# A two-layer decoder on one core: unrolled expert slots of 47 tiles, norms in two parts, and the store inside the combining stage

## The chip, the cores and the metric

The kernel runs on one core of a Trainium2 chip. The metric is the device time of one execution in microseconds, the median of the runs. TensorE's full clock is 2.4 GHz, and the profile gives the granted share of it.

## The reference, cut to what matters

The input `x` is 4 batches of 512 tokens with 512 features. Six sublayers follow one another, each added to its input and layer-normed: causal attention, cross attention, a ternary-weight feed-forward net, causal attention again, a graph layer, and a mixture of experts. The last two are what the change touches.

```
# graph layer (L1_xattn), added to x, then the norm
sim  = (h Wq)(h Wk)^T scaled;  thr = 153rd largest of each row
A    = sigmoid(sim) * (sim >= thr);  A = (A + A^T) / 2
x    = layernorm(x + (1 - gamma) * x + gamma * A)
# mixture of experts (L1_ffn), 16 experts of width 256, top 2
combine[n, e] = the two renormed shares of token n
for e in range(16):
    out += combine[:, e] * ((silu(x Wu[e]) * (x Wg[e])) @ Wd[e])
out += shared expert;  x = layernorm(x + out)
```

## The kernel before

`X` holds the 2048 tokens in SBUF as 16 tiles of 128 tokens by 512 features. `build` runs the stages one after another; each is a block in which every engine has its own instruction list in program order, with semaphores between the engines, and each ends with a barrier.

**The graph stage** (`stage_graph`) ends with a loop over the 4 batches. ScalarE makes four sigmoids (line 1546) and scales four tiles of X (1550); VectorE masks (1584); TensorE transposes the masked tiles (1522); VectorE adds tile and transpose (1591), adds that to X (1597) and takes the moments with `bn_stats` (1600). After the loop VectorE runs the 25 small dependent steps of `emit_rstd` (lines 64 to 77) for all 16 tiles at once, and then norms the 16 tiles (1605).

**The expert stage** (`stage_experts`) has three parts. `route_and_share` sorts the tokens by expert into tiles of 128 rows that each belong to one expert, and computes the shared expert. At most `SLOT_TILES` = 48 such tiles are there, and all of them are computed. `run_slots` runs over these 48 slots. For each one, GpSimd issues two indirect DMAs, of the tokens (`XG`, 128 rows of 2 KB, line 1986) and of the expert's weights (`RAW`, 128 rows of 12 KB, line 1988). Every fp32 product is made of three fp32r products: ScalarE copies the high part (`WH`, `XTH`, `HH`), an engine subtracts it from the raw value to get the low part (`WL`, `XTL`, `HL`), and TensorE multiplies high by high, low by high and high by low. The low part of the up weights comes in two halves: VectorE does the first (2089), GpSimd the second (1993). In one slot TensorE does 8 up products (2144), the 2 transposes of H of the slot before (2159), the last 4 up products, the 4 transposes of the next slot's tokens (2132), and the 6 down products of the slot before (2178).

The order of the other engines in turn t is: GpSimd waits until VectorE has copied the two row numbers of slot t+3 into `PICK` (2080, 2081) and until `down_lo` of slot t-1, issues the two DMAs of slot t+3, and subtracts for slot t+1. VectorE copies the row numbers, subtracts for the up weights of t+1, and makes `HL` of t-1 (2104), `XTL` of t+1 (2085), `H` of t (2109), the copy of the result `YS` of t-1 out of PSUM (2118) and the low part of the down weights of t (2121). ScalarE copies the up weights of t+1 (2060), `HH` of t-1 (2064), `XTH` of t+1 (2036), takes the silu of t (2069) and copies the down weights of t (2072). SyncE stores `YS` to `y_rows` in HBM (2027). RAW, XG and YS are rings of 4 buffers, the other tiles rings of 2 or 1. The first 4 and the last 5 turns are written out, and the 40 between them are a hardware loop (`Fori`) of 4 turns.

**`combine_slots`** gathers for each of the 16 token tiles the two result rows by indirect DMA (2207, a ring of 4), and VectorE adds them to X with their shares (2216) and takes the moments (2219); then come the 25 steps and the 16 norms (2224), all on VectorE. After the barrier `store_x` writes X with one 4 MB DMA (2268).

Of the kernel before, what the change touches and what calls it, by code (L numbers as in the profile page):

```python
# [4 lines left out]
F32 = mybir.dt.float32  # L5
# [8 lines left out]
P = 128  # L14
NB = 4
# [64 lines left out]
def emit_rstd(nc, step, stats, mean, var, y, a):  # L80

    for inst in rstd_steps(nc, stats, mean, var, y, a):
        step(inst)

# [1385 lines left out]
def stage_graph(nc, X, C, A, GR):  # L1470
# [10 lines left out]
    with ctx:  # L1481
# [16 lines left out]
        mean, var, rstd, tmp = (small(n, NTILE) for n in ("mean", "var", "rstd", "tmp"))  # L1498
# [3 lines left out]
                 "sigm xs masked turned summed halved z_done stat norm between")  # L1502
# [24 lines left out]
        def _(act):  # L1527
# [14 lines left out]
            with act.Fori(0, NB) as b:  # L1542
                act.wait_ge(q["masked"], b * NT)
                act.sem_inc(q["between"], 1)
                for i in range(NT):
                    ac.activation(SIGM[:, i, :], SIM[:, b * NT + i, :], ACT.Sigmoid).then_inc(q["sigm"], 1)
                act.wait_ge(q["z_done"], b * NT)
                act.sem_inc(q["between"], 1)
                for i in range(NT):
                    ac.activation(XS[:, i, :], XF[:, b * NT + i, :], ACT.Identity, scale=g2[:, 0:1]).then_inc(q["xs"], 1)  # L1550

        @block.vector
        def _(dve):
# [26 lines left out]
            with dve.Fori(0, NB) as b:  # L1580
                dve.wait_ge(q["turned"], b * 2)
                for i in range(NT):
                    dve.wait_ge(q["sigm"], b * NT + i + 1)
                    ve.scalar_tensor_tensor(out=L[:, i, :], in0=SIM[:, b * NT + i, :], scalar=low[:, bass.ds(b * NT + i, 1)],  # L1584
                                            in1=SIGM[:, i, :], op0=ALU.is_ge, op1=ALU.mult).then_inc(q["masked"], 1)
                for v in range(2):
                    dve.wait_ge(q["turned"], b * 2 + v + 1)
                    dve.wait_ge(q["masked"], b * NT + NT)
                    if v == 0:
# [11 lines left out]
            dve.wait_ge(q["stat"], NTILE)  # L1601
            fin = Steps(dve, q["norm"], 0, RSTD_STEPS + NTILE)
# [4 lines left out]
            fin.done()  # L1607

def stage_experts(nc, X, C, A):  # L1610
# [7 lines left out]
    SLOT_TILES = 2 * NTILE + NE  # L1618
    ctx = ExitStack()
    with ctx:  # L1620
# [13 lines left out]
        combine_slots(nc, X, T)  # L1634
# [289 lines left out]
def run_slots(nc, X, C, A, T, F, SLOT_TILES):  # L1924

    RING = 4
    TURNS = SLOT_TILES // RING  # L1930
    UGW, DW = KC * 2 * F, 2 * D
    pe, ve, ac, gp = nc.tensor, nc.vector, nc.scalar, nc.gpsimd
    ctx = ExitStack()
    with ctx:
# [4 lines left out]
        def places(n, count, w, dtype):  # L1939
# [5 lines left out]
        YS = places("YS", RING, D, F32)  # L1945
        PICK = places("PICK", RING, 2, U32)
# [13 lines left out]
        q = {n: sem(n) for n in ("picked xt_full x_hi x_lo up_hi down_hi up_lo up_lo_pool down_lo "  # L1960
                                 "u_full silu_done h_made ht_full h_hi h_lo y_full y_taken between").split()}
        x_in, w_in, y_out = ([sem(f"{n}{i}") for i in range(RING)] for n in ("x_in", "w_in", "y_out"))

# [5 lines left out]
        def run(eng, step):  # L1969

            for i in range(RING):
                step(i, i)
            with eng.Fori(1, TURNS - 1) as j:
                for i in range(RING):
                    step(j * RING + i, i)
            for i in range(RING + 1):
                step((TURNS - 1) * RING + i, i)

        def has(t, lo, hi):
            return not isinstance(t, int) or lo <= t <= hi  # L1980

        @block.gpsimd
        def _(pool):
            def fetch(t, i):
                i = i % RING
                pool.indirect_dma_start(out=XG[i], out_offset=None, in_=T["x_rows"],  # L1986
# [361 lines left out]
```

## Time and profile before

| | |
|---|---|
| median of 3 runs | 2813.01 us (2809.75 to 2814.63) |
| the profiled execution: its own time | 2814.64 us |
| its span | 2812.7 us, 34294 instructions |
| TensorE busy, matmuls | 2066.3 us (73%) |
| its instructions | 12308 matmuls, 12308 weight loads |
| VectorE busy | 1822.6 us (65%) |
| ScalarE busy | 1217.9 us (43%) |
| GpSimd busy | 801.8 us (29%) |
| DMA, mean over the span | 95 GB/s |
| mean granted clock of TensorE | 0.858 |

The span is cut by stages: the graph loop and its norms lie at 2078 to 2150 us, routing and the shared expert at 2150 to 2389, the 48 slots at 2389 to 2736, the combination at 2736 to 2799, and the store at 2800 to 2813. The shares of busy time are means over stages with different limits; the rows that follow are read stage by stage. A busy time counts what the engine spent in its instructions, a wait for a shared resource included.

### The profile page before, as it was taken

Reading aid. Unit: us, or ns where it says so; the run is one execution under the profiler, and the core shown is the slowest. Engines: PE = TensorE matmul, PEld = TensorE weight load, DVE = VectorE, ACT = ScalarE, POOL = GpSimd, SP = SyncE. Lnnn points to the kernel's source line nnn. Section 1 sums busy time; section 2 is a strip of 40 time slices with the busy share of each in tenths; the row PEclk is TensorE's granted clock in tenths of the full one; section 3 lists DMA queues with packets and bytes.
Section 4 is the critical chain, followed back from the end, with each engine's and each line's share of the span. In section 5 each row is a group of like instructions: output and inputs, shape, how many; then the busy total and the mean of one; then the engine's idle time right before and its main releaser. Section 6 shows DMA issues by size and latency. Waiting matters only on the chain. (4 is left out here: it accounts for less than half of the span.)

```text
span 2812.7 us, 34294 instructions
## 1 busy us (share of the span) xinstructions
PE 2066.3 (73%) x12308; PEld 1398.0 (50%) x12308; DVE 1822.6 (65%) x2851; ACT 1217.9 (43%) x2168; POOL 801.8 (29%) x712
## 2 busy tenths in 40 slices
PE   5999997386877886899847999994014589677760
PEld 4778775122222223555526777772003477555540
DVE  3456555476767757899963555654885433788876
ACT  2332222285556563677762322321862021556540
POOL 1211322106577511121111212131000130666654
PEclk8999998589889888999967999997555599999995
DMA  4422221655244204000013223221002000899965
GB/s 142 98 56 59 57 58 23 180 173 144 90 127 121 61 12 170 1 1 1 1 38 98 64 50 69 52 62 60 0 0 107 1 1 0 308 307 303 305 223 164
DMA packets 84875, 266.48 MB, mean 95 GB/s; under 512 B 17488, under 2 KB 19024, under 8 KB 73600
## 3 DMA queue, kind: packets, MB, share of 16 engines
q0 software_dynamic: 29856, 153.33, 18.2%
q1 hardware_dynamic: 53856, 111.01, 13.9%
q8 instruction: 89, 1.46, 0.2%
q10 hardware_dynamic: 1024, 0.26, 0.0%
q14 instruction: 50, 0.41, 0.0%
HBM read 171.70 MB, written 41.99 MB: 76 GB/s over the span
## 5 line engine op out<-in xcount | busy, mean ns | idle before, releaser
L875 DVE TENSOR_REDUCE x_negm<-x_M 128x2 f32<-128x1024 f32 x256 | 309.3, 1223 | 115.4 <-PE x_M L935 114.9
L824 ACT ACTIVATE x_PT<-x_T 128x512 f32<-128x512 f32 x512 | 280.2, 598 | 210.8 <-PE x_T L955 206.0
L317 ACT ACTIVATE L_attn_PT<-L_attn_T 128x512 f32<-128x512 f32 x320 | 175.4, 595 | 357.9 <-PE L_attn_T L519 357.7
L387 DVE TENSOR_REDUCE L_attn_negm<-L_attn_M 128x2 f32<-128x1024 f32 (+1 forms) x192 | 191.8, 1041 | 56.5 <-PE L_attn_M L500 56.2
L224 POOL DMA_DIRECT2D L_attn_QKS<-L_attn_HL x64 | 34.9, 546 | 598.0 <-ACT L_attn_HL L302 564.3
L955 PE MATMUL x_T<-x_QS,x_KS 49*128 49x512 f32 x512 | 144.0, 559 | 64.0 <-ACT x_PT L824 43.7
L517 PE MATMUL L_attn_T<-L_attn_QKS 97*128 97x256 f32 (+3 forms) x512 | 164.6, 383 | 10.2 <-DMA L_attn_QKS<-L_attn_mT 7.9
L964 PE MATMUL x_O<-x_PT,x_V 128*32 128x512 f32 x1024 | 160.7, 704 | 7.6 <-issue 7.6
L955 PEld LDWEIGHTS x_T<-x_QS,x_KS 49*128 49x128 f32 x512 | 53.0, 204 | 217.5 <-ACT x_PT L824 135.9
L935 PE MATMUL x_M<-x_KS,x_QS 48*128 48x512 f32 x512 | 120.7, 468 | 42.8 <-DMA x_QS<-x_xl 23.3
L498 PE MATMUL L_attn_M<-L_attn_QKS 96*128 96x384 f32 (+2 forms) x384 | 134.8, 420 | 19.2 <-DVE L_attn_XTL L361 11.5
L1522 PE MATMUL graph_P<-ident,graph_L 128*128 128x128 f32 x64 | 15.7, 428 | 173.0 <-DVE graph_L L1584 167.8
L2060 ACT ACTIVATE slots_WH<-slots_RAW 128x1024 fp32r<-128x1024 f32 x94 | 94.6, 1054 | 100.3 <-DMA slots_RAW<-in_experts,slots_PICK 100.3
L2121 DVE TENSOR_TENSOR slots_WL<-slots_RAW,slots_WH 128x1024 fp32r<-128x1024 f32 x48 | 130.9, 2726 | 0.2 <-ACT slots_WH L2072 0.2
L434 PE MATMUL L_attn_M<-L_attn_XTH,L_attn_WH 128*128 128x512 f32 x256 | 109.1, 426 | 16.3 <-DVE L_attn_XTL L361 16.3
L519 PE MATMUL L_attn_T<-mask_kq,identr 128*128 128x128 f32 x512 | 120.4, 247 | 0.0
L1993 POOL TENSOR_TENSOR slots_WL<-slots_RAW,slots_WH 128x1024 fp32r<-128x1024 f32 x48 | 116.3, 2423 | 10.5 <-ACT slots_WH L2060 5.6
L1534 ACT ACTIVATE graph_seen_a<-graph_SIM,graph_mid 128x512 bf16<-128x512 f32 x128 | 90.5, 708 | 59.1 <-DMA graph_SIM<-graph_sim 39.8
L517 PEld LDWEIGHTS L_attn_T<-L_attn_QKS 97*128 97x128 f32 x512 | 104.8, 205 | 17.0 <-DMA L_attn_QKS<-L_attn_mT 9.1
L405 DVE RECIPROCAL L_attn_AQ<-L_attn_DEN 128x512 f32<-128x512 f32 x32 | 107.2, 3349 | 7.1 <-PE L_attn_O L537 7.1
L434 PE MATMUL L_attn_M<-L_attn_XTH,L_attn_WL 128*128 128x512 f32 x256 | 106.4, 416 | 0.0
L1986 POOL DMA_INDIRECT slots_XG<-moe_x_rows,slots_PICK x48 | 48.6, 1012 | 201.7 <-DVE slots_PICK L2081 200.9
(377 smaller groups left out, 5711.9 us busy)
## 6 DMA issues: line engine op xcount, KB each, us to landing
L_attn_QKS<-L_attn_HL SPq DMA_DIRECT2D x192, 128.0 KB, 4.7
L_attn_QKS<-L_attn_HL POOLq DMA_DIRECT2D x192, 128.0 KB, 4.1
moe_y_rows<-slots_YS SPq DMA_DIRECT2D x48, 256.0 KB, 7.6
x_WRAW<-in_w_gateT POOLq DMA_DIRECT2D x8, 1024.0 KB, 7.5
x_QS<-x_xh SPq DMA_DIRECT2D x128, 64.0 KB, 2.4
x_WRAW<-in_w_upT POOLq DMA_DIRECT2D x8, 1024.0 KB, 5.6
x_WRAW<-in_w_downT POOLq DMA_DIRECT2D x8, 1024.0 KB, 5.9
ffn_w<-x_WTER POOLq DMA_DIRECT2D x12, 512.0 KB, 3.6
```

The source lines that it names most:

```text
L317: ac.activation(PT[:, s, bank], T[:, bank], ACT.Exp, scale=SCALE).then_inc(t_free, 1)
L387: last = ve.tensor_reduce(negm[:, g % 2, h0:h0 + nh, i], src, AX.X, ALU.max, negate=True)
L434: inst = pe.matmul(out, lhs(a, k), rhs(a, k), start=(n == 0), stop=(n == len(passes) - 1))
L498: pe.matmul(m[:, c:c + w], QKS[0:R, r, 0, h, P * i:P * (i + 1)], QKS[0:R, r, 1, h, 0:w], start=True, stop=False)
L517: pe.matmul(T[:, c:c + w], QKS[0:R + 1, r, 1, h, P * j:P * (j + 1)], QKS[0:R + 1, r, 0, h, P * j:S], start=True, stop=False)
L519: last = pe.matmul(T[:, c:c + P], C["identr"][:], C["mask_kq"][:], start=False, stop=True)
L824: ac.activation(PT[:, s // 4, head(s), :], T[(STEPS_S * g + s) % 3][:], ACT.Exp, scale=SCALE).then_inc(t_free, 1)
L875: ve.tensor_reduce(negm[:, g % 2, u // 4:4:2, u % 4], m[:].rearrange("p (r k) -> p r k", r=2), AX.X, ALU.max, negate=True).then_inc(m_free, 1)
L935: last = pe.matmul(m[:, BANK * r:BANK * (r + 1)], QS[rows, g % 4, u // 4, P * (u % 4):P * (u % 4 + 1)], KS[rows, g % KV, :], start=True, s ...
L955: pe.matmul(T[(STEPS_S * g + s) % 3][:], KS[rows, g % KV, P * j:P * (j + 1)], QS[rows, g % 4, head(s) % 2, :], start=True, stop=True).then ...
L964: last = pe.matmul(O[VW * h:VW * (h + 1), :], V[:, (g // KV) % 2, j, g % KV, :], PT[:, j, h, :], start=(j == 0), stop=(j == NT - 1))
L2121: ve.tensor_tensor(WL[i % 2][:, DOWN], RAW[i][:, DOWN], WH[i % 2][:, DOWN].bitcast(F32), ALU.subtract).then_inc(q["down_lo"], 1)
```

## The change

- `run_slots`: the loop is written out for all slots, and `SLOT_TILES` is 47. GpSimd only issues DMAs; the row numbers are taken in place from `slot_token` and `weight_row`, without `PICK`. RAW and XG are rings of 6, and slot t is fetched once slot t-6 has been read (`down_lo`, `up_lo`). VectorE does both halves of the up weights' low part. ScalarE copies the result out of PSUM (`take_y`). SyncE's stores have constant addresses.
- `stage_graph`: the loop over batches is written out; the moments of the first 12 tiles are turned into mean, rstd and `shift` = -mean*rstd inside the last batch, those of the last 4 tiles at the end. ScalarE norms the first 14 tiles and VectorE the last 2.
- `combine_slots`: the same in two parts, and SyncE stores each batch once it is normed, the last one in two halves of 0.5 MB. `store_x` isn't called any more.

```diff
@@ stage_graph
+            for b in range(NB):
...
+                if b == NB - 1:
+                    moments(0, 0, EARLY)
...
-            emit_rstd(nc, fin, stats[:], mean[:], var[:], rstd[:], tmp[:])
-            for t in range(NTILE):
-                fin(ve.tensor_scalar(XF[:, t, :], XF[:, t, :], mean[:, t:t + 1], rstd[:, t:t + 1],
-                                     ALU.subtract, ALU.mult))
+            moments(1, EARLY, NTILE)
+            last = Steps(dve, q["between"], 0, NT // 2)
+            for t in range(EARLY + NT // 2, NTILE):
+                last(ve.tensor_scalar(XF[:, t, :], XF[:, t, :], mean[:, t:t + 1], rstd[:, t:t + 1],
+                                      ALU.subtract, ALU.mult))
@@ run_slots
-    RING = 4
+    RING, LAST = 6, SLOT_TILES - 1
@@ run_slots, GpSimd
+            for t in range(SLOT_TILES):
+                n = t % RING
+                if t >= RING:
+                    pool.wait_ge(down_lo, t - RING + 1)
+                    pool.wait_ge(up_lo, 2 * (t - RING + 1))
+                pool.indirect_dma_start(out=XG[n], out_offset=None, in_=T["x_rows"],
+                                        in_offset=bass.IndirectOffsetOnAxis(T["slot_token"][:, t:t + 1], 0)
+                                        ).then_inc(x_in[n], 16)
+                pool.indirect_dma_start(out=RAW[n], out_offset=None, in_=weights,
+                                        in_offset=bass.IndirectOffsetOnAxis(T["weight_row"][:, t:t + 1], 0)
+                                        ).then_inc(w_in[n], 16)
@@ run_slots, ScalarE
+            for t in range(SLOT_TILES + 2):
+                if t < LAST:
+                    up_weights(t + 1)
+                if 1 <= t <= SLOT_TILES:
+                    act.wait_ge(ht_full, t)
+                    ac.activation(HH[:], HT[:, 0:F], ACT.Copy).then_inc(h_hi, 1)
+                if t >= 2:
+                    take_y(t - 2)
+                if t < LAST:
+                    turned(t + 1)
+                if t <= LAST:
+                    act.wait_ge(u_full, t + 1)
+                    ac.activation(SU[t % 2], U[t % 2][:, 0:F], ACT.Silu).then_inc(silu_done, 1)
+                    if t >= 2:
+                        act.wait_ge(y_full, t - 1)
+                    ac.activation(WH[t % 2][:, DOWN], RAW[t % RING][:, DOWN], ACT.Copy).then_inc(down_hi, 1)
@@ run_slots, VectorE
+            for t in range(SLOT_TILES + 1):
+                if t < LAST:
+                    up_rest(t + 1, 0)
+                if t >= 1:
+                    dve.wait_ge(h_hi, t)
+                    ve.tensor_tensor(HL[:], HT[:, 0:F], HH[:].bitcast(F32), ALU.subtract).then_inc(h_lo, 1)
+                if t < LAST:
+                    up_rest(t + 1, 1)
+                    turned_rest(t + 1)
+                if t <= LAST:
+                    dve.wait_ge(silu_done, t + 1)
+                    ve.tensor_tensor(H[t % 2], SU[t % 2], U[t % 2][:, F:], ALU.mult).then_inc(h_made, 1)
+                    dve.wait_ge(down_hi, t + 1)
+                    ve.tensor_tensor(WL[t % 2][:, DOWN], RAW[t % RING][:, DOWN], WH[t % 2][:, DOWN].bitcast(F32),
+                                     ALU.subtract).then_inc(down_lo, 1)
@@ combine_slots, VectorE
             for t in range(NTILE):
+                if t == EARLY:
+                    moments(0, 0, EARLY)
...
+            moments(1, EARLY, NTILE)
+            for t in range(EARLY + NT // 2, NTILE):
+                ve.tensor_scalar(XF[:, t, :], XF[:, t, :], mean[:, t:t + 1], rstd[:, t:t + 1],
+                                 ALU.subtract, ALU.mult).then_inc(applied_v, 1)
@@ combine_slots, ScalarE
+            act.wait_ge(shifted, 1)
+            for t in range(EARLY):
+                norm_tile(t)
+            act.wait_ge(shifted, 2)
+            for t in range(EARLY, EARLY + NT // 2):
+                norm_tile(t)
@@ combine_slots, SyncE
+            for b in range(NB - 1):
+                sp.wait_ge(applied_a, NT * (b + 1))
+                sp.dma_start(out[:, b, :, :], X[:, b, :, :]).then_inc(x_out, 16)
+            sp.wait_ge(applied_a, EARLY + NT // 2)
+            sp.dma_start(out[:, NB - 1, 0:NT // 2, :], X[:, NB - 1, 0:NT // 2, :]).then_inc(x_out, 16)
+            sp.wait_ge(applied_v, NT // 2)
+            sp.dma_start(out[:, NB - 1, NT // 2:, :], X[:, NB - 1, NT // 2:, :]).then_inc(x_out, 16)
```

`EARLY` is 12. `moments(part, lo, hi)` waits for the `bn_stats` of tiles below `hi`, runs `emit_rstd` and one more step, `emit_shift`, on tiles `lo` to `hi`, and releases ScalarE. `norm_tile(t)` is one activation with scale `rstd` and bias `shift`, in place. TensorE's order in a slot stays as it was.

## Rows read from the trace of the kernel before

**Rows 1.** Windows: length, busy PE PEld DVE ACT POOL, PEclk, DMA share, GB/s.
```profile
2403.00:2407.00 4.00, 4.00 (x12) 3.10 (x12) 1.10 (x1) 2.01 (x2) 2.78 (x4) 0.60 1.01 427
2407.00:2411.00 4.00, 2.50 (x14) 1.90 (x13) 2.56 (x7) 3.27 (x5) 2.34 (x1) 1.00 1.01 390
2430.00:2700.00 270.00, 209.61 (x944) 157.12 (x944) 236.69 (x316) 159.85 (x236) 169.33 (x118) 1.00 0.91 305
2801.00:2811.00 10.00, 0.00 (x0) 0.00 (x0) 0.00 (x0) 0.00 (x0) 0.00 (x0) 0.50 1.03 386
```

**Rows 2.** Waits of the engines from 2430 to 2700 us.
```profile
ACT slots_WH L2060 <- DMA slots_RAW<-in_experts,slots_PICK: 87.4, 39, 3.4
...
PE slots_Y L2178 <- DVE slots_HL L2104: 42.0, 39, 1.2
...
PE slots_U L2144 <- POOL slots_WL L1993: 18.2, 40, 0.5
```

**Rows 3.** Timeline of one slot: start, us, engine, line, operation.
```profile
2562.89 0.98 POOL L1986 DMA_INDIRECT slots_XG<-moe_x_rows,slots_PICK  x1 [2.20 <-DVE slots_PICK L2081]
...
2564.18 0.95 POOL L1988 DMA_INDIRECT slots_RAW<-in_experts,slots_PICK  x1 [0.30 <-issue]
...
2565.15 2.38 POOL L1993 TENSOR_TENSOR slots_WL<-slots_RAW,slots_WH 128x1024 fp32r<-128x1024 f32 x1
...
2565.72 2.90 DVE L2121 TENSOR_TENSOR slots_WL<-slots_RAW,slots_WH 128x1024 fp32r<-128x1024 f32 x1
...
2568.55 0.14 DVE L2080 COPY slots_PICK<-moe_slot_token 128x1 uint32 x1
```

**Rows 4.** Groups by form, 2430 to 2700 us: busy, mean ns, idle before.
```profile
L2089 DVE TENSOR_TENSOR slots_WL<-slots_RAW,slots_WH 128x1024 fp32r<-128x1024 f32 x40 | 48.4, 1210 | 0.0
...
L2118 DVE COPY slots_YS<-slots_Y 128x512 f32<-128x512 f32 x39 | 27.0, 692 | 33.1 <-PE slots_Y L2178 33.1
...
L2036 ACT ACTIVATE slots_XTH<-slots_XT 128x512 fp32r<-128x512 f32 x40 | 23.8, 595 | 22.7 <-PE slots_XT L2132 22.3
```

**Rows 5.** Timeline: TensorE's first up products of slots 1, 2 and 47.
```profile
2409.20 1.17 PE L2144 MATMUL slots_U<-slots_WH,slots_XTH 128*128 128x512 f32 x4 [1.50 <-DVE slots_XTL L2085]
...
2414.33 1.16 PE L2144 MATMUL slots_U<-slots_WH,slots_XTH 128*128 128x512 f32 x4
...
2722.15 1.09 PE L2144 MATMUL slots_U<-slots_WH,slots_XTH 128*128 128x512 f32 x4
```

**Rows 6.** DMA issues, 2430 to 2700 us; last number: median us to landing.
```profile
slots_RAW<-in_experts,slots_PICK POOLq DMA_INDIRECT x39, 9.3
```

**Rows 7.** The tile YS over the whole span: landing of its stores.
```profile
DMA to landing us min/median/max: 2.0/7.6/9.6
```

**Rows 8.** The page's third part: instruction blocks fetched by DMA.
```profile
q8 instruction: 89, 1.46, 0.2%
```

**Rows 9.** Timeline of the combination and the store.
```profile
2770.93 1.54 DVE L2216 SCALAR_TENSOR_TENSOR X<-combine_YG,moe_share,X 128x512 f32<-128x512 f32 x2 [0.31 <-DMA combine_YG<-moe_y_rows,moe_slot]
...
2772.50 0.69 DVE L2219 BATCH_NORM_STATS2 combine_stats<-X 128x6 f32<-128x512 f32 x1
...
2783.69 0.69 DVE L2219 BATCH_NORM_STATS2 combine_stats<-X 128x6 f32<-128x512 f32 x1
...
2799.90 0.39 SPq L2268 DMA_DIRECT2D out_x<-X  x1
```

**Rows 10.** Timeline of the last batch of the graph stage and its norms.
```profile
2120.47 2.56 ACT L1550 ACTIVATE graph_XS<-X,graph_g 128x512 f32 x4 [7.86 <-DVE X L1597]
2121.15 2.74 DVE L1584 SCALAR_TENSOR_TENSOR graph_L<-graph_SIM,graph_low,graph_SIGM 128x512 f32<-128x512 f32 x4
...
2126.02 1.23 DVE L1591 TENSOR_TENSOR graph_SUM<-graph_P,graph_L 128x1024 f32<-128x1024 f32 x1 [2.13 <-PE graph_P L1522]
...
2134.83 0.18 DVE L64 TENSOR_TENSOR graph_mean<-graph_stats 128x16 f32<-128x16 f32 x1
...
2140.08 9.28 DVE L1605 TENSOR_SCALAR X<-X,graph_mean,graph_rstd 128x512 f32<-128x512 f32 x16
```

More of the change, by code:

```diff
@@ L83, in emit_rstd, with emit_shift @@
         step(inst)
+def emit_shift(nc, step, mean, rstd, shift):
+    step(nc.vector.scalar_tensor_tensor(out=shift, in0=mean, scalar=-1.0, in1=rstd, op0=ALU.mult, op1=ALU.mult))
 def moment_steps(nc, t, z):
@@ L1944, in run_slots @@
         XG = places("XG", RING, D, F32)
[L1945 to L1946 removed]
+        YS = places("YS", 4, D, F32)
         WH = places("WH", 2, UGW + DW, F32R)
@@ L2018, in _ @@
         @block.sync
         def _(sp):
-            def step(t, i):
-                if has(t, 1, SLOT_TILES):
-                    sp.wait_ge(q["y_taken"], t)
-                    if not isinstance(t, int):
-                        sp.sem_inc(q["between"], 1)
-                    n = (i - 1) % RING
-                    rows = slice(P * (t - 1), P * t) if isinstance(t, int) else bass.ds((t - 1) * P, P)
-                    sp.dma_start(T["y_rows"][rows], YS[n]).then_inc(y_out[n], 16)
-            run(sp, step)
@@ L2073, in _, with up_weights, turned, take_y @@
-            run(act, step)
+            def up_weights(t):
+                act.wait_ge(w_in[t % RING], 16 * (t // RING + 1))
+                if t >= 2:
+                    act.wait_ge(u_full, t - 1)
+                for part in PARTS:
+                    ac.activation(WH[t % 2][:, part], RAW[t % RING][:, part], ACT.Copy).then_inc(up_hi, 1)
+            def turned(t):
+                act.wait_ge(xt_full, t + 1)
+                ac.activation(XTH[t % 2], XT[:], ACT.Copy).then_inc(x_hi, 1)
+            def take_y(t):
+                act.wait_ge(y_full, t + 1)
+                if t >= 4:
+                    act.wait_ge(y_out[t % 4], 16 * (t // 4))
+                ac.activation(YS[t % 4], Y[t % 2][:], ACT.Copy).then_inc(y_taken, 1)
@@ L2123, in _, with turned_rest, up_rest @@
-            run(dve, step)
+            def turned_rest(t):
+                dve.wait_ge(x_hi, t + 1)
+                ve.tensor_tensor(XTL[t % 2], XT[:], XTH[t % 2].bitcast(F32), ALU.subtract).then_inc(x_lo, 1)
+            def up_rest(t, part):
+                dve.wait_ge(up_hi, 2 * t + part + 1)
+                cols = PARTS[part]
+                ve.tensor_tensor(WL[t % 2][:, cols], RAW[t % RING][:, cols], WH[t % 2][:, cols].bitcast(F32),
+                                 ALU.subtract).then_inc(up_lo, 1)
@@ L2180, in step, with combine_slots @@
                             n += 1
-                    last.then_inc(q["y_full"], 1)
-            run(t_, step)
-def combine_slots(nc, X, T):
+                    last.then_inc(y_full, 1)
+def combine_slots(nc, X, T, out):
     NTILE, RING = NB * NT, 4
-    ve = nc.vector
+    EARLY = NTILE - NT
+    ve, ac = nc.vector, nc.scalar
     ctx = ExitStack()
@@ L2296, in build @@
             if s == "M":
-                stage_experts(nc, X, C, A)
-        store_x(nc, X, out.rearrange("b (i p) d -> p b i d", p=P))
+                stage_experts(nc, X, C, A, out_rows)
+        if "M" not in stages:
+            store_x(nc, X, out_rows)
 def layout(inputs):
```

301 lines of the change are left out of this document (111 added, 190 removed).

## The prediction, made before the changed kernel ran

> **What bounds the kernel now.** I read the page's slices first, then the stages by window, then the waits, the timeline and the groups of the slot loop. The stages run one after another, so each is its own problem, and three are touched. The big one is the 48 slots. TensorE goes from slot 1's first up product at 2409.20 to slot 47's at 2722.15 [rows 5], 46 steps of 6.80 us; from 2430 to 2700 a slot takes 6.87 us, which makes 39.3 of them. No resource is full there: in 270 us TensorE is busy 209.6, ScalarE 159.9, and VectorE 236.7 in name only [rows 1]. The timeline shows what paces it [rows 3]. GpSimd waits 2.20 us for VectorE's PICK, issues two DMAs (0.98 and 0.95), and subtracts for 2.38 us, until 2567.53. VectorE's down subtract begins inside that time and takes 2.90 us, though the same shape takes 1.21 on line 2089 [rows 4]; it ends at 2568.62, just 1.1 us after GpSimd's. So it is held until GpSimd is done, and costs 1.69 more. The next PICK starts at 2568.55, and GpSimd's next issue waits for it. That is a ring through two engines: PICK, two issues, GpSimd's subtract, VectorE's held subtract, PICK. TensorE pays for it with 42.0/39 = 1.08 us a slot waiting for HL, which stands behind VectorE's held work, and 18.2/40 = 0.46 for GpSimd's half [rows 2]. ScalarE's 87.4/39 = 2.2 us of waiting for RAW [rows 2] is the same ring seen from the DMA: RAW is issued late and lands 9.3 us after its issue [rows 6].
>
> **The slots, part by part.** GpSimd's subtract, PICK and the hold go; the ring is cut. What limits next?
> TensorE: its list is unchanged. 6.87 - 1.08 - 0.46 = 5.33 us, and the step from slot 1 to slot 2, before the hold sets in, took 2414.33 - 2409.20 = 5.13 [rows 5]. Floor 5.13.
> VectorE: 236.69/39.3 = 6.02 us a slot [rows 1]; less the hold 1.69, the YS copy 0.69 [rows 4] and two picks (about 0.2 [rows 3]); plus one subtract of 1.21 [rows 4]: 4.65.
> ScalarE: 159.85/39.3 = 4.07 [rows 1], plus `take_y`. That form isn't in the trace; XTH is the same size from PSUM, 0.595 [rows 4]: 4.66. From below it can't be free, from above VectorE's copy is 0.69.
> GpSimd: 0.98 + 0.95 + two gaps of 0.30 = 3.2 at most, with nothing behind it but itself.
> DMA: a slot moves 305 GB/s x 6.87 us = 2.095 MB [rows 1]. With three weight loads queued the engines moved 427 and then 390 GB/s, the big store 386 [rows 1]: 4.91, 5.37 and 5.43 us a slot.
> With the ring of 6, slot t is fetched when slot t-6 is done, some five slots ahead of use, so the 9.3 us of landing hide, and the DMA queues never run dry. So TensorE (5.13) and the DMA (about 5.4) are the next bounds, and VectorE and ScalarE have 0.5 us of slack each. The latter matters: HL now stands behind one unheld subtract of 1.21, and XTL behind HL and the second one. The path from TensorE's transposes of H through HH, HL, the second subtract and XTL to the next up products is about 0.4 + 0.4 + 0.4 + 1.2 + 0.7 us, which is as long as TensorE's own work in that time (5.13 less the 8 up products at about 0.23 each). It fits with nothing to spare. I take 5.45 us, from the sustained DMA rates; the ends are 5.13 and, below, 6.25.
> Steps: before 46 x 6.80 = 312.95; after 45 x 5.45 = 245.25 (one slot less). **Gain 67.7 us.** The first slot is paced by its weights and the half clock of TensorE as before, and the last one's tail stays: nothing for both. SyncE's stores keep their order; they are hidden behind three slots of the ring.
> The unrolling itself I price at nothing: the first four turns and the last five were written out already, and the step from slot 1 to 2, in that part, is the fastest. What it costs if that fails is a rival.
>
> **The combination and the store.** Tile 11 is added from 2770.93 and its moments end at 2773.19 [rows 9]. Then come `moments(0)`, 26 dependent steps. In the graph stage 25 of them took 2140.08 - 2134.83 = 5.25 [rows 10], so 26 take 5.46: until 2778.65. Four tiles of 1.54 + 0.69 = 2.23 follow; their gathers were issued meanwhile, since the ring of 4 doesn't wait for them: 2787.6, against 2784.38 before. `moments(1)`: 2793.1. Then VectorE norms two tiles at 9.28/16 = 0.58 [rows 10] while ScalarE does two at 2.56/4 = 0.64 [rows 10]: both end by 2794.4. ScalarE's 12 early tiles (7.7 us from 2778.7) end at 2786.4, under VectorE's adding, and each batch's 1 MB (2.7 us at 386 GB/s) is stored by 2790. What is left behind 2794.4 is 1 MB: 2.7 us, plus a fixed part. The 4 MB store went from 2799.90 to the span's end at 2812.7, 12.8 us, of which 4.19 MB at 386 GB/s is 10.9; so 1.9 is fixed. The barrier between the last norm (about 2799.0) and the issue, 0.9 us, now lies behind the store. 2794.4 + 0.1 + 2.7 + 1.9 + 0.9 = 2800.0 to 2800.6 with the second issue. **Gain 12.2 us.**
>
> **The graph stage.** Its last mask ends at 2123.89. 26 steps: 2129.35, of which 2.13 us filled VectorE's wait for TensorE [rows 10]. From the first sum at 2126.02 to the steps at 2134.83 are 8.8 us, so 2138.2; `moments(1)` 2143.6; two norms 2145.0, against 2149.36. ScalarE's 12 tiles lie under it (2129.4 to 2137.1). **Gain 4.4 us.** The written-out loop gains nothing: no gap stands between batches on VectorE.
>
> **Sum.** 67.7 + 12.2 + 4.4 = 84.3. The profiled execution (span 2812.7, own time 2814.64) would come to a span of 2728.4 and a time of 2730.3; against the median of 2813.01 that is **2728.7 us**.
>
> **Rivals.**
> *Reads and writes together don't reach 386 GB/s.* In the even part the DMA share was already 0.91 at 305 GB/s [rows 1]. If those packets are as slow with full queues, the limit is 305/0.91 = 335 GB/s, a slot takes 6.25 us, the slots gain 312.95 - 281.3 = 31.7, and the time is 2813.0 - 48.3 = 2765. For it: the 386 and 390 were rates of writes alone and reads alone. The trace has gone over it, 427 and 390 GB/s in [rows 1].
> *The stores starve.* A YS store lands in 2.0 us when nothing else moves and in 7.6 as a rule [rows 7]: it waits behind weight packets. If a store has to wait for all that is queued, then with a ring of 6 that is 5 x 1.835 MB at 390 GB/s, 23.5 us, plus 2.0. YS has 4 places, so a slot can't go below 25.5/4 = 6.4 us: gain 25 + 16.6, 2771. Before, at most one or two loads were queued, so the trace can't exclude it. The skill (the same page, Queues, rings and completion order) says that an engine alternates between queues packet by packet; by that rule the store waits for one load's share and this rival falls.
> *The ring isn't the bound.* Another cycle over the engines, such as the tight path above, keeps the step at 6.8. Then one slot less (6.8), 0.15 or so, and 16.6: 2789. Against it: the 5.13 us step.
> *Slower.* The written-out lists have to be fetched. 89 blocks of 16.4 KB were [rows 8], mostly under low DMA load. If they are TensorE's, 1.46 MB over its 24,616 instructions (the table) is an estimate of 59 B each; with 48 a slot (2 x 944/39.3 [rows 1]), 47 slots are 8 blocks. If each is fetched only when needed, and waits for the whole backlog of 23.5 us, that is 8 x 23.5 = 188 us: 2917. It decides from 84.3/8 = 10.5 us a block. Against it: no stall shows at blocks fetched so far, so they come ahead of need, and a block lasts nearly six slots.
>
> **How the numbers follow.** The forecast (5.13 to 5.75 us a slot, 2714 to 2742) gets 0.60, the slow DMA (2742 to 2769) 0.22, starving stores 0.09, the unmoved bound 0.05, slower 0.04. The lower end of the range is the TensorE floor less 2 us for the two tails: 2712. Upward, 2762 leaves out the slowest third of the second case and the three others, about 0.2 in all. A measurement of this kernel can tell from no change what exceeds about 0.2%, 5.6 us: faster 0.95, same 0.01, slower 0.04.
>
> **What would show it.** After, VectorE's down subtract takes 1.21 us, not 2.90. TensorE's first up products come 5.45 us apart, and its waits for HL and GpSimd's half shrink from 1.54 to about 0.3 us. DMA runs at some 385 GB/s with a share near 1; if the share is 1 at 335 to 350 GB/s the second case holds; if ScalarE waits in `take_y` for a store, the third; if TensorE has idle time of 10 us with a q8 block in it, the last. The span ends about 30 us after the combination's tile 11 is added, not 42. The prediction is wrong if VectorE and ScalarE, with half a microsecond of slack, delay each other more than TensorE's list can hide.

## The result, and the profile after

The changed kernel takes **2701.65 us** (median of 4 runs, 2691.3 to 2702.86) against 2813.82 (4 runs, 2809.75 to 2814.71): 112 us less by the medians. The ratio of the runs, 0.9616 with a 95% interval of 0.9594 to 0.9638, makes it 108 us (102 to 114). The forecast was 2729, with a range of 2712 to 2762. The direction held, and so did what the prediction said of the kernel before; but the next bound was TensorE's own list and not the DMA, the gain was 28 us more than forecast (24 by the ratio), and the time lies below the range. All medians here are of executions in the usual, fast state; one of the four of "after, half on GpSimd" took 3019.73 us at a granted clock of 0.701 and is left out.

The profiled execution took 2691.3 us (span 2689.6), the fastest of the four. Part of its lead is not the change's: TensorE's first instruction of the graph stage starts at 2066.18 us and before at 2082.94, and all stages ahead of it are the same code. In the 14 traces of this study with that same code it starts anywhere from 2066 to 2088, and TensorE's mean granted clock up to there lies between 0.860 and 0.873. So the parts are read as lengths between two instructions of the same stages. In the last column is what the prediction's steps give.

| part | before | after | gain | forecast |
|---|---|---|---|---|
| graph stage, TensorE's first to next stage's first | 67.47 | 60.18 | 7.3 | 4.4 |
| routing and shared expert | 243.50 | 241.46 | 2.0 | 0 |
| slot 1 to the last slot, first up products | 312.95 | 230.97 | 82.0 | 67.7 |
| slot 0 to 1, and last slot to the end of its YS copy | 16.31 | 14.92 | 1.4 | 0 |
| first gather to the end of the span | 77.06 | 63.57 | 13.5 | 12.2 |
| sum | | | 106.2 | 84.3 |

The sum of 106 lies inside the interval of 102 to 114; the 2 us to the ratio's 108 and the 6 to the medians' difference are no more than the untouched stages vary.

The slots first. These are the windows of the kernel after that answer to [rows 1] (after the window and its length come the busy times of PE, PEld, DVE, ACT and POOL, then the granted clock, the DMA share and GB/s):

```profile
2377.00:2400.00 23.00, 21.29 (x96) 16.26 (x95) 19.62 (x24) 18.63 (x27) 10.44 (x9) 0.95 1.02 423
2400.00:2580.00 180.00, 177.59 (x844) 135.72 (x843) 172.14 (x211) 161.06 (x246) 101.97 (x71) 1.00 1.01 417
2580.00:2600.00 20.00, 19.72 (x95) 15.02 (x94) 19.09 (x25) 17.82 (x28) 8.34 (x6) 1.00 1.00 413
```

TensorE is busy 177.6 us of 180 instead of 209.6 of 270, and the DMA moves 417 GB/s for 180 us on end. Its first up products of slots 1, 2 and 46, for [rows 5]:

```profile
2382.67 1.16 PE L2101 MATMUL slots_U<-slots_WH,slots_XTH 128*128 128x512 f32 x4 [1.50 <-DVE slots_XTL L2058]
...
2387.81 0.47 PE L2101 MATMUL slots_U<-slots_WH,slots_XTH 128*128 128x512 f32 x1
...
2613.64 0.47 PE L2101 MATMUL slots_U<-slots_WH,slots_XTH 128*128 128x512 f32 x1
```

That is 230.97 us for 45 steps, 5.13 each, and every one is between 5.11 and 5.14. The waits from 2400 to 2580 us, all of them, against [rows 2]:

```profile
POOL slots_XG L2001 <- DVE slots_WL L2082: 69.3, 36, 1.9
ACT slots_XTH L2027 <- PE slots_XT L2092: 17.1, 35, 0.5
PEld slots_U L2101 <- issue: 16.5, 35, 0.5
POOL slots_RAW L2004 <- issue: 10.7, 35, 0.3
DVE slots_WL L2082 <- ACT slots_WH L2052: 7.1, 35, 0.2
```

No wait of TensorE's matmuls is left in the list, and ScalarE no longer waits for RAW. What stands first, GpSimd's 1.9 us a slot, is the wait for a place in the ring; nobody is late for it, since five further slots are already loaded or on their way. The groups of the same stretch, for [rows 4]:

```profile
L2063 DVE TENSOR_TENSOR slots_WL<-slots_RAW,slots_WH 128x1024 fp32r<-128x1024 f32 x71 | 86.4, 1217 | 0.0
...
L2001 POOL DMA_INDIRECT slots_XG<-moe_x_rows,moe_slot_token x36 | 60.6, 1684 | 69.3 <-DVE slots_WL L2082 69.3
L2082 DVE TENSOR_TENSOR slots_WL<-slots_RAW,slots_WH 128x1024 fp32r<-128x1024 f32 x35 | 42.9, 1226 | 7.1 <-ACT slots_WH L2052 7.1
L2004 POOL DMA_INDIRECT slots_RAW<-in_experts,moe_weight_row x35 | 42.7, 1219 | 10.7 <-issue 10.7
...
L2033 ACT ACTIVATE slots_YS<-slots_Y 128x512 f32<-128x512 f32 x35 | 20.8, 594 | 0.0
```

VectorE's down subtract takes 1.23 us, not 2.90, and the result's copy 0.594 on ScalarE (forecast 0.595). Now GpSimd pays: its issues take 1.68 and 1.22 us, where they took 0.98 and 0.95 [rows 3].

The combination, for [rows 9]:

```profile
2661.01 1.54 DVE L2183 SCALAR_TENSOR_TENSOR X<-combine_YG,moe_share,X 128x512 f32<-128x512 f32 x2 [0.67 <-DMA combine_YG<-moe_y_rows,moe_slot]
...
2668.90 8.57 ACT L2195 ACTIVATE X<-X,combine_shift,combine_rstd 128x512 f32<-128x512 f32 x12 [46.71 <-DVEq L2176]
...
2677.04 0.69 DVE L2186 BATCH_NORM_STATS2 combine_stats<-X 128x6 f32<-128x512 f32 x1
...
2683.01 1.52 ACT L2195 ACTIVATE X<-X,combine_shift,combine_rstd 128x512 f32<-128x512 f32 x2 [5.53 <-DVEq L2176]
...
2684.97 0.47 SPq L2213 DMA_DIRECT2D out_x<-X  x1
```

From tile 11's addition to the end it is 28.6 us instead of 41.8.

### The profile page after: what moved, and what is told of

It is laid out like the page before. It is cut to its first block and busy times, and to the rows that moved or that the text cites. A ratio compares the mean times of both kernels' runs of the same rounds, so it can differ in the third digit from the quotient of the medians.

```text
span 2689.6 us, 33324 instructions
## 1 busy us (share of the span) xinstructions
PE 2040.0 (76%) x12284; PEld 1381.2 (51%) x12284; DVE 1763.9 (66%) x2775; ACT 1257.8 (47%) x2237; POOL 719.8 (27%) x662
## 5 line engine op out<-in xcount | busy, mean ns | idle before, releaser
L960 PE MATMUL x_T<-x_QS,x_KS 49*128 49x512 f32 x512 | 143.1, 555 | 60.2 <-ACT x_PT L829 43.3
L2001 POOL DMA_INDIRECT slots_XG<-moe_x_rows,moe_slot_token x47 | 75.4, 1605 | 188.3 <-POOLq L48 104.2
L2063 DVE TENSOR_TENSOR slots_WL<-slots_RAW,slots_WH 128x1024 fp32r<-128x1024 f32 x94 | 114.3, 1218 | 13.4 <-ACT slots_WH L2023 13.4
L524 PEld LDWEIGHTS L_attn_T<-mask_kq,identr 128*128 128x128 f32 x512 | 105.0, 205 | 0.2
```

Of the source, the lines that this page charges most:

```text
L524: last = pe.matmul(T[:, c:c + P], C["identr"][:], C["mask_kq"][:], start=False, stop=True)
L960: pe.matmul(T[(STEPS_S * g + s) % 3][:], KS[rows, g % KV, P * j:P * (j + 1)], QS[rows, g % 4, head(s) % 2, :], start=True, stop=True).then ...
L2063: ve.tensor_tensor(WL[t % 2][:, cols], RAW[t % RING][:, cols], WH[t % 2][:, cols].bitcast(F32), ALU.subtract).then_inc(up_lo, 1)
```

## The experiments

The experiments ran in three groups, each on one chip with its own runs of the kernel before; that median stands in the third column, and times of different groups are compared by ratios and by lengths in the traces alone. "Step" is always the mean from slot 1's first up product to the last slot's. "Fewer products" and "tokens fetched twice" have two executions each, so they are read by their steps.

| kernel | time, us | before in its group | step, us | ratio to before, 95% |
|---|---|---|---|---|
| before | 2813.82 | | 6.80 | |
| after | 2701.65 | 2813.82 | 5.13 | 0.9594 to 0.9638 |
| slots only | 2725.28 | 2804.03 | 5.13 | 0.9671 to 0.9747 |
| combination only | 2792.02 | 2804.03 | | 0.9942 to 0.9982 |
| graph stage only | 2800.58 | 2804.03 | | 0.9943 to 0.9988 |
| slot loop written out only | 2805.17 | 2804.03 | 6.85 | 0.9972 to 1.0017 |
| half to VectorE only | 2790.09 | 2811.93 | 6.34 | 0.9901 to 0.9967 |
| after, half on GpSimd | 2749.98 | 2811.93 | 6.27 | 0.9759 to 0.9853 |
| after, rings of 4 | 2735.80 | 2811.93 | 6.08 | 0.9695 to 0.9770 |
| after, YS copy on VectorE | 2704.86 | 2811.93 | 5.26 | 0.9592 to 0.9660 |
| after, rings of 5 | 2728.67 | 2831.19 | 5.12 | 0.9608 to 0.9650 |
| after, fewer products | 2717.57 | 2831.19 | 4.94 | 0.9551 to 0.9634 |
| after, tokens fetched twice | 2752.46 | 2831.19 | 5.74 | 0.9693 to 0.9738 |
| graph loop written out only | 2829.16 | 2831.19 | 6.81 | 0.9969 to 1.0004 |

### The three parts, each alone

Each is the kernel before with one function taken from the kernel after.

```diff
-    SLOT_TILES = 2 * NTILE + NE
+    SLOT_TILES = 2 * NTILE + NE - 1
```

> The kernel before with the new run_slots and 47 slots; graph stage, combination and final store as before. Theory A: the three parts are independent, so this part has what the slots gained in the full change: a step of 5.13 us between TensorE's first up products (the length of TensorE's own list), 312.95 - 45 x 5.13 = 82 us from slot 1 to the last, 1.2 more in the tail; in all about 83 us less than before, to about 2730. Theory B, as the prediction had it: the DMA paces at 5.45 us, 68 us less, and the rest of the surplus came from elsewhere. Theory C: the shorter combination and graph stage help the slots too, and this kernel gains clearly less than the 97 us that slots, combination and store gained together less 13.4.

Measured: 231.01 us from slot 1 to the last, 5.13 a step; the ratio of 0.9709 makes 82 us less (71 to 92). Theory A. The slots' 5.13 doesn't depend on the other parts.

> The kernel before with only the combination changed: 12 tiles' moments early, norms on ScalarE for 14 tiles, each batch stored as it is normed, no 4 MB store at the end. The prediction said 12.2 us less; by the trace of the kernel after, first gather to the end of the span went from 77.0 to 63.6, 13.4 less. Theory A: 12 to 13.5 us less. Theory B, part of those 13.4 belongs to a shorter tail of the slots or to another state of the gathers: under 11.

Measured: from the first gather to the end of the span 63.65 us, before 77.06: 13.4 less. The time's own interval, 5 to 16 us less, can't separate the theories, the length can. Theory A.

> The kernel before with only the graph stage changed: loop over the batches written out, norms in two parts on two engines. The prediction said 4.4 us less, with nothing from writing out the loop; the trace after shows the stage 7.3 us shorter. Theory A: 7 us less, of which some 0.8 us for each of the four batches is from the written-out loop. Theory B: 4.4 less, and the rest of the 7.3 is how TensorE's clock fell in that stage.

Measured: the graph stage takes 60.2 us, as in the full change, so 7.3 less; the ratio makes the whole kernel 10 us less (3 to 16). What made up the 7.3 is taken apart by the last experiment.

### Is it the loop, the subtract or the ring?

```diff
-            for i in range(RING):
-                step(i, i)
-            with eng.Fori(1, TURNS - 1) as j:
-                for i in range(RING):
-                    step(j * RING + i, i)
-            for i in range(RING + 1):
-                step((TURNS - 1) * RING + i, i)
+            for t in range(SLOT_TILES + 1):
+                step(t, t - RING * min(t // RING, TURNS - 1))
```

> The kernel before with the 40 looped slots written out and nothing else: still 48 slots, rings of 4, the row numbers copied to PICK, GpSimd's half of the subtract. Theory A, the ring PICK, two issues, GpSimd's subtract, VectorE's held subtract is the pace: the step stays at 6.8 us and the time within 6 us of before. Theory B, the loop itself (waits against counted registers, its branch) sets a part of the pace, as the graph stage's shorter batches suggest, some 0.1 us for each wait: then the step falls by 0.2 to 1 us, 8 to 40 us less.

Measured: step 6.85, ratio 0.9995. Theory A: writing the slots out gives nothing by itself. The mean is 0.05 us higher than before because of a few slow steps, one of 9.61 us with a late load; the median step is 6.85 in both.

The second takes GpSimd's half away from it, in the kernel before:

```diff
@@ GpSimd
-                if has(t, 0, SLOT_TILES - 2):
-                    rest(t + 1, i + 1)
@@ VectorE, after HL of t-1
+                    up_rest2(t + 1, i + 1)
```

> The kernel before with one thing changed: GpSimd's half of the subtract of the up weights goes to VectorE. The loop, PICK, the rings of 4, 48 slots and the YS copy on VectorE stay. Theory A, VectorE's subtract was held by GpSimd's, and this closed the ring: with both on VectorE its work is 6.02 - 1.69 + 1.21 = 5.54 us a slot, its subtracts take 1.21 us each, and the step falls from 6.80 to about 5.55, 59 us less, with VectorE now the bound. Theory B, the late issues (PICK, ring of 4) are a bound of their own: RAW still arrives late, the step stays above 6.3.

Measured: step 6.34, 18 us less than before (9 to 28). VectorE's subtracts do take 1.21 us, so the hold is gone, but the step is far from theory A's 5.55 and just above the 6.3 of theory B. Theory B. The single steps swing between 5.4 and 9.6 us, and the loads come late:

```profile
ACT slots_WH L2052 <- DMA slots_RAW<-in_experts,slots_PICK: 90.3, 42, 4.1
```

These are 2.15 us a slot from 2430 to 2700 us, as much as in [rows 2]. So a second bound stood right behind the first. Whether it is PICK or the depth of the ring, this run doesn't tell; the rings of 4 below show that the depth alone is such a bound.

The third is the opposite: rings of 6 and no PICK as in the kernel after, and GpSimd subtracts again.

```diff
+            for t in range(SLOT_TILES + RING - 1):
+                if t >= RING - 1:
+                    rest(t - RING + 1)
@@ VectorE
-                    up_rest(t + 1, 1)
```

> The kernel after with GpSimd doing the second half of the subtract again; rings of 6, no PICK, written out. GpSimd: 0.98 + 0.95 + 0.3 + 2.38 = 4.6 us a slot, VectorE 4.65 - 1.21 + 1.69 = 5.1 if its subtract is held as before, and nobody is above TensorE's 5.13 by much. Theory A, the hold costs only where GpSimd's issue hangs on VectorE: with the ring cut the step is 5.13 to 5.5 us, 0 to 17 us more than after. Theory B, the hold alone makes the path through HL and XTL too long: 5.8 or more, over 30 us more than after.

Measured: step 6.27, 1.14 above after, and over 6 from the first steps on; 53 us above after by the ratios (0.9806 against 0.9616). Theory B. The groups from 2430 to 2580 us:

```profile
L1999 POOL TENSOR_TENSOR slots_WL<-slots_RAW,slots_WH 128x1024 fp32r<-128x1024 f32 x24 | 62.1, 2589 | 0.5
L2074 DVE TENSOR_TENSOR slots_WL<-slots_RAW,slots_WH 128x1024 fp32r<-128x1024 f32 x24 | 55.4, 2307 | 0.0
L2091 DVE TENSOR_TENSOR slots_WL<-slots_RAW,slots_WH 128x1024 fp32r<-128x1024 f32 x23 | 50.3, 2185 | 4.1 <-ACT slots_WH L2063 3.6
```

The hold now falls on either of VectorE's two subtracts, and both average over 2.1 us against 1.2. No load is late here, though the DMA moves 332 GB/s at a share of 0.94. The Trainium skill (SBUF — State Buffer, Who interferes with whom) says that VectorE and GpSimd share one pair of SBUF ports, that a VectorE instruction with both inputs in SBUF contends for it with a GpSimd instruction that reads SBUF, and that the one that comes second waits until the first is done. By that rule the hold is there as long as both subtract, and the trace agrees: 2.2 to 2.3 us instead of 1.2.

The fourth is the kernel after with `RING = 4` in place of 6.

> The kernel after with RAW and XG rings of 4 in place of 6. In the kernel after RAW lands 10.8 us (16.7 at most) after its issue. With 4 places a load is issued at most 3 slots ahead of its use, less the time in which the slot is read: 15.4 - 5.1 = 10.3 us at a step of 5.13. Theory A: a shorter queue also shortens the landing (9.3 us before), the step stays at 5.13 and the time within 4 us of after. Theory B: the landing doesn't fit, some slots wait for RAW, the step is 5.4 to 6.2, 12 to 50 us more than after.

Measured: step 6.08, theory B: 42 us more over the slots, and 33 by the ratio (0.9733 against after's 0.9616). Steps of 5.13 alternate with steps of up to 9.4. First the window and the waits from 2430 to 2580 us, then the DMA in 40 slices from 2470 to 2492 us:

```profile
2430.00:2580.00 150.00, 132.90 (x594) 100.46 (x594) 120.88 (x149) 112.42 (x173) 62.22 (x49) 0.96 0.93 341
...
ACT slots_WH L2023 <- DMA slots_RAW<-in_experts,moe_weight_row: 24.9, 18, 4.3
...
GB/s 246 261 320 331 421 410 406 406 473 413 447 358 425 421 458 439 387 469 424 350 317 183 89 115 153 305 246 0 156 443 469 417 421 465 417 324 302 249 373 216
```

The queue runs dry: the slices from 2481.5 to 2486 us have 0 to 305 GB/s, after GpSimd has waited 6.3 us for a place. RAW lands 9.9 us after its issue in the median (7.9 to 11.1), and the packets are slower as well: 0.93 of the engines' time for 341 GB/s, against 1.01 for 417 with full queues, 13% more time a byte. On paper 4 places are enough (9.9 for the landing, 2.3 from the release to RAW's issue, some 6.5 of use in the kernel after, which is 18.7 of 4 x 5.13 = 20.5), so there is some 2 us to spare for a transfer that swings by 3. That this swing is what uses it up is a reading of these rows and not shown by a run of its own. What is shown is the price of the depth: 6.08 against 5.13 us a step, with neither PICK nor hold in either kernel.

The same with `RING = 5`:

> The kernel after with rings of 5 for RAW and XG. With 4 places the queue ran dry in most slots, the step was 6.05 and the time about 34 us over after. Theory A, the pace is a matter of places times the step against load, wait and use of a place: one place more adds 5.13 us for a landing of 9 to 11 us, the queue never runs dry, and the step is 5.13, the time within 3 us of after. Theory B, the landing time grows with the depth (11.8 us at 6), so that 5 places still leave stalls: 5.2 to 5.5, 3 to 17 us over after.

Measured: step 5.12, and the window is full again, 148.0 us of TensorE in 150:

```profile
2430.00:2580.00 150.00, 148.00 (x705) 113.31 (x704) 143.51 (x176) 134.56 (x205) 84.42 (x59) 1.00 1.01 409
```

Theory A: five places do it, the sixth gives nothing. (The traces have 6.08 where the expectation says 6.05, and a median landing of 10.9 us where it says 11.8.) (Its group's chip was slower: the stage of the shared expert lasts 264 us there, below. Its ratio of 0.9629 lies in after's interval.)

### How full are the others?

```diff
@@ ScalarE
-                if t >= 2:
-                    take_y(t - 2)
@@ VectorE, before H of t
+                    ve.tensor_copy(YS[(t - 1) % 4], Y[(t - 1) % 2][:]).then_inc(y_taken, 1)
```

> The kernel after with the copy of the result YS on VectorE again (0.69 us) in place of ScalarE (0.59). Theory A, VectorE becomes the bound: 4.7 to 4.9 + 0.69 = 5.4 to 5.55 us a slot, 12 to 20 us more than after. Theory B, TensorE's list is the bound with room to spare on all others: 5.13 to 5.2, at most 3 us more.

Measured: step 5.26; 3 us more than after by the ratio, 5.9 by the steps. VectorE is busy for all of the 180 us, with no gap at all:

```profile
2400.00:2580.00 180.00, 175.75 (x822) 133.23 (x821) 180.00 (x240) 140.50 (x206) 96.86 (x68) 1.00 1.02 409
```

Theory A was right on the bound and wrong on the size: it took up to 4.9 us of busy time as work. Saturated, VectorE does a slot in 5.26, the copy's 0.67 among them, so its work in the kernel after is about 4.6.

The next leaves out the products with the weights' low part:

```diff
-                    ups = [(xp, wp, k) for xp, wp in ((XTH[i], WH[i]), (XTL[i], WH[i]), (XTH[i], WL[i]))
+                    ups = [(xp, wp, k) for xp, wp in ((XTH[i], WH[i]), (XTL[i], WH[i]))
...
-                    for hp, wp in ((HH, WH[r]), (HL, WH[r]), (HH, WL[r])):
+                    for hp, wp in ((HH, WH[r]), (HL, WH[r])):
```

> The kernel after without the products of the weights' low part (high part of the tokens or of H by WL); left out are 4 of the 12 up products of a slot and 2 of its 6 down products, so the output is less exact. All copies, subtracts and transfers stay. It shows which bound is next below TensorE's 5.13 us. By the runs so far VectorE saturated comes to 5.27 - 0.67 = 4.60 us a slot, ScalarE to 161.06/35.1 = 4.59, and the loads' landing time in the kernel after fell by 0.19 us from slot to slot, so that the DMA needs 5.13 - 0.19 = 4.94. Theory A: TensorE's list alone sets 5.13; the step falls to 4.9 to 5.0, and the DMA is the next bound: 6 to 11 us less than after. Theory B, something of the same length, the path over HL and XTL, sets 5.13 too: then the step stays at 5.1. Theory C: the DMA is no bound either, 4.7 or less.

Measured: 4.67 us a step for five of the first steps, while loads issued earlier lie ready, then 4.95. In the first of these two windows VectorE is busy all the time; the second, and the wait that has come back, are from 2450 to 2600 us:

```profile
2432.00:2455.00 23.00, 19.55 (x90) 13.84 (x90) 23.00 (x31) 22.35 (x36) 13.89 (x11) 1.00 1.01 419
...
2450.00:2600.00 150.00, 118.73 (x542) 83.08 (x541) 145.90 (x183) 135.32 (x212) 89.69 (x61) 1.00 1.02 424
...
ACT slots_WH L2023 <- DMA slots_RAW<-in_experts,moe_weight_row: 14.6, 29, 0.9
```

Theory A, with both sizes (the slots take 8.9 us less than in the kernel after): TensorE's own list is what makes 5.13; the DMA comes next at 4.95 (424 GB/s), then VectorE at 4.67, and ScalarE below that.

```diff
+                pool.indirect_dma_start(out=XG2[n], out_offset=None, in_=T["x_rows"],
+                                        in_offset=bass.IndirectOffsetOnAxis(T["slot_token"][:, t:t + 1], 0)
+                                        ).then_inc(x_in[n], 16)
```

> The kernel after with each slot's token rows fetched a second time, into a buffer that nobody reads: 0.262 MB more, 2.357 MB a slot in place of 2.095, and one more DMA on GpSimd (about 1.7 us). The output is unchanged. It measures what the DMA can sustain with full queues. At 386 GB/s, the rate that the prediction took, a slot would take 6.11 us, 44 us more than after; at the 424 GB/s that the falling landing time gives (2.095 MB in 4.94 us) 5.56 us, 19 us more; if the step stays at 5.13, the rate is over 459. GpSimd with three issues comes to at most 4.6 us.

Measured: most steps are close to 5.62 (mean 5.74), 27.5 us more than after over the slots, and ScalarE waits for RAW in each slot. The same window:

```profile
2450.00:2600.00 150.00, 137.99 (x624) 100.91 (x623) 125.35 (x157) 116.65 (x182) 89.11 (x78) 1.00 1.02 417
```

2.357 MB in 5.62 us is 419 GB/s. Two kernels with different loads meet the same limit of 417 to 424 GB/s, so this is the DMA's rate here, reads and writes together.

### The graph stage's loop

```diff
-            with act.Fori(0, NB) as b:
-                act.wait_ge(q["masked"], b * NT)
-                act.sem_inc(q["between"], 1)
+            for b in range(NB):
+                if b:
+                    act.wait_ge(q["masked"], b * NT)
```

and the same for VectorE and TensorE.

> The kernel before with only the graph stage's loop over the four batches written out; norms as before. The prediction said that this gains nothing. Of the stage's 7.3 us (60.18 against 67.49 from TensorE's first instruction in it to its first in the next stage) 4.4 were foreseen for the norms. Theory A, the written-out loop has shorter waits: the stage is 2.5 to 3.2 us shorter. Theory B, nothing: the stage stays at 67.5 and all 7.3 are from the norms in two parts. The 2.2 us that the next stage gained in both kernels with the new graph stage, while TensorE's idle time before it fell from 21 to 13 us, should be absent here, since the norms leave TensorE idle for about 21 us again.

Measured: the stage takes 64.51 us, 3.0 less than 67.49. Theory A. VectorE's masks of two batches that follow each other, first before, then with the loop written out:

```profile
2093.79 2.74 DVE L1584 SCALAR_TENSOR_TENSOR graph_L<-graph_SIM,graph_low,graph_SIGM 128x512 f32<-128x512 f32 x4
...
2107.48 2.74 DVE L1584 SCALAR_TENSOR_TENSOR graph_L<-graph_SIM,graph_low,graph_SIGM 128x512 f32<-128x512 f32 x4
```

```profile
2082.88 2.72 DVE L1585 SCALAR_TENSOR_TENSOR graph_L<-graph_SIM,graph_low,graph_SIGM 128x512 f32<-128x512 f32 x4
...
2095.79 0.73 DVE L1585 SCALAR_TENSOR_TENSOR graph_L<-graph_SIM,graph_low,graph_SIGM 128x512 f32<-128x512 f32 x1
```

A batch takes 12.91 us instead of 13.69, 0.78 less. VectorE's instructions are as long as before; wherever one waits for the one just ahead of it (a sum or an addition, then what reads it) it starts about 0.1 us sooner. In the loop both the waits and the addresses of the tiles hang on the loop's counter; this run changes the two together and doesn't tell which of them costs the 0.1 us. The rest of the stage's gain, 64.51 - 60.18 = 4.3, is the norms in two parts.

The next stage's gain is no part of either. At 61.65 us after that stage's start VectorE makes its third pick of an expert in the kernel before; it is 62.33 in this one, and 59.84 and 60.21 in the two kernels with the new norms (graph stage only, and after). Part of this is visible in the clock. Here is the idle time at the graph stage's end, and then two stretches early in the next stage; first before, then after:

```profile
2134.00:2150.00 16.00, 0.00 (x0) 0.00 (x0) 13.82 (x42) 0.00 (x0) 0.00 (x0) 0.50 0.00 0
...
2153.60:2157.00 3.40, 1.65 (x13) 1.17 (x12) 2.40 (x3) 1.87 (x3) 0.00 (x0) 1.00 0.97 394
2157.00:2160.40 3.40, 2.81 (x14) 2.41 (x13) 2.04 (x2) 1.79 (x2) 0.00 (x0) 0.50 1.01 337
```

```profile
2113.00:2126.00 13.00, 0.52 (x3) 0.12 (x1) 10.65 (x36) 7.21 (x11) 0.00 (x0) 0.50 0.00 0
...
2130.20:2133.60 3.40, 2.09 (x16) 1.71 (x16) 2.35 (x2) 1.87 (x2) 0.00 (x0) 1.00 1.00 423
2133.60:2137.00 3.40, 2.12 (x17) 1.71 (x16) 2.35 (x2) 1.98 (x3) 0.00 (x0) 1.00 1.00 301
```

TensorE is granted half its clock (1.2 GHz) in both idle stretches and gets the full 2.4 GHz 3.2 us after the stage's first matmul before, 3.9 us after it in the kernel after. But before, the clock falls back to half for 3.4 us, after a stretch in which TensorE was busy 1.65 of 3.40 us, and 16 transposes then take 2.88 us instead of 2.22; after, it stays up for 13.6 us. With only the graph loop written out it falls back for 6.9 us, which fits the 62.33. All six traces with the old norms have such a fall, none of the eight with the new ones. TensorE's idle time ahead of the stage is 21 us in the first six and 13 in the others, so it goes with the fall; but two kernels with 21 us have falls of 3.4 and 6.9 us, so the idle time alone doesn't say how long it lasts. What decides it is open.

## Why the prediction was right, and where it was wrong

**What bound the slots: right.** "A ring through two engines": with GpSimd's half back in the kernel after, the step is 6.27 and the hold is there. But the ring was one of two bounds of nearly one height. Either alone gives little (6.80 to 6.34 with the half moved; 6.27 with the ring of 6 and no PICK, in a kernel that also has the YS copy on ScalarE), both together give 5.13. The prediction put the late RAW down to the ring over the two engines and didn't price the depth by itself; it had both edits in the sum, so this cost it nothing.

**The size of the step: this is where it failed.** "I take 5.45 us, from the sustained DMA rates." That made the DMA the pace after the change; the runs show TensorE's own list at 5.13. The rates of 390 and 386 GB/s were no limits. The first came from a window of 4 us in which the loads began, the other from a store alone; in the kernel after the DMA moves 417 for 180 us, and where it does set the pace it moves 417 to 424, which is 4.95 us a slot. The floor named beside it, TensorE's 5.13 from one step of [rows 5], is the step, to the hundredth. 45 x (5.45 - 5.13) = 14.3 us. This alone would put the time at 2714, still inside the range, whose lower end of 2712 is that floor less 2 us for the tails; the time came out below it through the terms that the prediction put at nothing or too low, the last four of this section.

**Reads and writes together (335 GB/s, 2765): refuted.** The share of 0.91 at 305 GB/s was no limit: the kernel after moves 417 at 1.01, while the rings of 4 have 341 at 0.93 and GpSimd's half 332 at 0.94. A byte takes longer in queues that aren't full, as its counter-argument had it; that the packets wait there for a first answer is its explanation, and no run shows it. The limit of about 358 GB/s for a core that the Trainium skill has (DMA: Bandwidth & Descriptors, Specifications) is passed by 60 here. The Trainium skill (the same page, Bandwidth, Measured) gives 425 GB/s for a load of 16 MB with the other core of the pair idle. This kernel runs on one core, and the measured 417 to 424 are close to that.

**Starving stores: refuted.** A store would have had to take 25.5 us. This is YS's landing after, over the whole span, for [rows 7]:

```profile
DMA to landing us min/median/max: 2.0/7.0/9.9
```

**VectorE 4.65, ScalarE 4.66 a slot:** right; VectorE saturated does a slot in 4.6 to 4.67, and ScalarE in at most 4.67. The tight path over HL and XTL hides, as forecast.

**Fetching of written-out lists:** no stall, since every step of the slots lies between 5.11 and 5.14; blocks in the whole span, for [rows 8]:

```profile
q8 instruction: 96, 1.57, 0.2%
```

**Nothing for the start and the tail:** 1.4 us too little. From the last slot's up products to the end of its YS copy it is 8.55 us and was 9.70.

**The combination: right within 1.3 us.** `moments(0)` takes 5.5 (forecast 5.46), the four tiles 8.8 (8.9), `moments(1)` 5.1 (5.46). The end is shorter than worked out: from the last issue at 2684.97 to the span's end 4.6 us, where 2.7 + 1.9 + 0.9 = 5.5 were counted.

**"The written-out loop gains nothing: no gap stands between batches on VectorE":** wrong by 3.0 us. The gaps are not between batches but between single instructions, 0.1 us each. The norms' 4.4 measured 4.3.

**Not seen at all:** 2.0 us in the next stage. 1.4 of them are there by VectorE's third pick of an expert, and TensorE's clock goes with them.

14.3 + 1.4 + 1.3 + 2.9 + 2.0 = 21.9 of the 28 us; the other 6 (2 by the ratio) lie within what the untouched stages vary.

## What to carry to other kernels

Take a step that the trace shows without its stall as the forecast (here a single one, 5.13, was right), and a transfer rate only from a stretch whose queues are full for many transfers; a rate of the first microseconds, or a busy share near 1 with queues that run dry, is no limit. Where a loop waits in two ways (an engine held by another, loads issued late), ask what each edit gives alone: here about 0.5 us each, and 1.7 together. A busy share says little on how full an engine or a queue is; the pace when it is the only bound does, and so does a landing time that rises or falls from slot to slot.

## What the runs showed that was not expected

- A DMA share of 1.01 is not the bound. In the kernel after the loads' landing falls through the stage, median 13.8 us from 2390 to 2420 and 9.5 from 2540 to 2570: the queue is being emptied faster than it is filled. With the loads at this pace of 5.13 us a slot the DMA needs 409 GB/s, as the rings of 5 show.
- VectorE's subtracts no longer wait for GpSimd, but GpSimd's issues of indirect DMAs stretch beside them, 0.98 to 1.68 and 0.95 to 1.22 us. In the same trace the eight issues that meet no subtract of WL take 0.95 us in the mean; the long ones have 1.37 us of subtracts beside them.
- A hardware loop costs about 0.1 us wherever a VectorE instruction waits for the one just ahead of it (graph loop, 0.78 us a batch), and nothing in the slots, where another bound covers it (ratio 0.9995).
- On the chip of the last group the shared expert's stage lasted 264 to 268 us, some 23 to 25 more, in all four kernels. For some 25 us of it TensorE started a matmul only every 0.7 to 2.8 us, its granted clock was at half for nearly all of that time (0.51 from 2260 to 2280 us with rings of 5), and no wait for data shows. What causes it is open; it is why that group's times are compared by their lengths and ratios alone.
